# Two-layer pair block on one core: three gate banks copied out before their sigmoids, second-norm roots earlier, third-norm roots regrouped

## The reference

```python
# layer 0
x    = layernorm(pair) * ln1_w + ln1_b
left = sigmoid(x @ left1) * (x @ left2);  right = sigmoid(x @ right1) * (x @ right2)
p    = einsum('nsre,nkre->nske', left, right)
p    = layernorm(p) * ln2_w + ln2_b
g    = sigmoid(x @ gate)
x1   = pair + einsum('nrse,ez->nsrz', p, out_w) * g
# layer 1
left = (x1 @ W_left + b_left) + (x1 @ W_eq + b_eq)
rsum = sum over r of (x1 @ W_right + b_right)
out  = left * rsum * sigmoid(x1 @ W_gate + b_gate)
out  = out @ W_out + b_out
return layernorm(out + x1) * ln_scale + ln_bias
```

## Time and profile before

| | us |
|---|---|
| median of 3 runs | 116.27 |
| lowest and highest | 115.69, 116.97 |
| the profiled execution, its own time | 115.33 |
| its span, first to last instruction | 113.5 |
| TensorE busy in the span | 89.4 |
| VectorE busy | 78.8 |
| ScalarE busy | 69.5 |
| GpSimd busy | 63.0 |

### The profile page before, as it was taken

How to read it: one execution, slowest core, us unless ns; L and a number is a source line. 1 busy time by engine, 2 the same in 40 slices (tenths; PEclk the granted TensorE clock), 3 DMA queues, 4 the chain that set the end, 5 groups by cost and what they waited for, 6 DMA issues and landing times.

```text
span 113.5 us, 1817 instructions
## 1 busy us (share of the span) xinstructions
PE 89.4 (79%) x566; PEld 69.4 (61%) x566; DVE 78.8 (69%) x279; ACT 69.5 (61%) x118; POOL 63.0 (56%) x78
## 2 busy tenths in 40 slices
PE   1965993299999899976399999999999998894000
PEld 1954572257777699634063598988779896894000
DVE  1528698949978800399694558667799897999910
ACT  0614788748786256672289747987995997731100
POOL 5037983699970000007466549298843969984800
PEclk9999599859999999999999999999999999999855
DMA  3589995000000000000000000000000014639796
GB/s 60 112 138 166 146 146 50 0 0 6 0 0 0 3 6 0 0 0 3 0 0 0 0 9 0 0 0 0 0 0 6 0 28 64 92 58 144 107 145 101
DMA packets 33484, 4.51 MB, mean 40 GB/s; under 512 B 33348, under 2 KB 33476, under 8 KB 33476
## 3 DMA queue, kind: packets, MB, share of 16 engines
q1 hardware_dynamic: 31632, 4.00, 26.9%
q10 hardware_dynamic: 1844, 0.41, 1.8%
HBM read 2.31 MB, written 2.10 MB: 39 GB/s over the span
## 4 chain that ended last, share of the span: by engine, by line
PE 53%; DVE 15%; ACT 8%; issue 8%; DMA 5%; POOL 3%; SPq 2%; DVEq 0%; POOLq 0%
PE bank L793 9%; PE bank L835 7%; PE bank L923 6%; DMA x_tok<-in_x 5%; PE bank L846 5%; PE bank L932 5%; PE bank L881 5%; PE bank L778 3%; PE bank L870 3%; DVE lr L709 3%; PE bank L895 3%; PE bank L898 3%; PE bank L896 3%; DVE stats L573 3%; DVE lr L588 3%
## 5 line engine op out<-in xcount | busy, mean ns | idle before, releaser
L351 POOL TENSOR_TENSOR t_tok<-p_sb,rstd 128x512 f32<-128x512 f32 x7 | 10.2, 1452 | 19.6 <-DVE rstd L659 19.6
L793 PE MATMUL bank<-lr_blk,xnT 64*128 64x256 f32 x128 | 18.2, 425 | 2.3 <-ACT xnT L420 2.1
L588 DVE TENSOR_TENSOR lr<-bank,sig_lr 128x512 f32<-128x512 f32 x16 | 15.9, 1042 | 3.7 <-ACT sig_lr L430 3.6
L359 POOL TENSOR_TENSOR x_low<-x1T,x_high 128x512 fp32r<-128x512 f32 x8 | 11.0, 1379 | 9.4 <-ACT x_high L489 9.4
L793 PEld LDWEIGHTS bank<-lr_blk,xnT 64*128 64x128 f32 x128 | 12.6, 200 | 5.9 <-POOL lr_blk L298 1.9
L653 DVE BATCH_NORM_STATS2 stats<-p_sb 128x6 f32<-128x64 f32 x64 | 8.6, 212 | 7.6 <-ACT p_sb L464 7.6
L430 ACT ACTIVATE sig_lr<-bank 128x512 f32<-128x512 f32 x16 | 9.6, 597 | 5.0 <-PE bank L793 5.0
L573 DVE BATCH_NORM_STATS2 stats<-x_tok 128x6 f32<-128x64 f32 x64 | 9.0, 214 | 3.5 <-DMA x_tok<-in_x 3.3
L375 POOL TENSOR_TENSOR sq<-lr,row_rep 128x512 f32<-128x512 f32 x7 | 9.8, 1400 | 2.0 <-DVE lr L712 2.0
L367 POOL TENSOR_TENSOR oT<-o_a,rsum 128x512 f32<-128x512 f32 x8 | 8.7, 1088 | 3.6 <-ACT rsum L493 2.0
L692 DVE SCALAR_TENSOR_TENSOR o_a<-bank,leq_bias,sig 128x512 f32<-128x512 f32 x8 | 6.0, 748 | 6.1 <-ACT sig L501 2.9
(11 more groups left out here) (99 smaller groups left out, 201.2 us busy)
## 6 DMA issues: line engine op xcount, KB each, us to landing
x_tok<-in_x SPq DMA_DIRECT2D x14, 128.0 KB, 4.3
out<-sq SPq DMA_DIRECT2D x7, 256.0 KB, 3.3
x_tok<-in_x SPq DMA_DIRECT2D x3, 64.0 KB, 2.6
w_rep<-in_weights ACTq DMA_DIRECT2D x1, 180.5 KB
out<-sq ACTq DMA_DIRECT2D x1, 128.0 KB, 4.6
out<-sq SPq DMA_DIRECT2D x1, 128.0 KB, 4.9
x_tok<-in_x ACTq DMA_DIRECT2D x1, 64.0 KB, 2.7
row_rep<-in_rows ACTq DMA_DIRECT2D x1, 32.0 KB, 5.2
```

The costliest lines, as they stand in the source:

```text
L351: nc.gpsimd.tensor_tensor(place(t_tok[:, c % 2], 0, SPC), even_first(p_sb[:, :, s]), even_first(rstd[:, 1:2, s]).to_broadcast([P, 2, SPC / ...
L359: nc.gpsimd.tensor_tensor(x1_low[:, c % 2], x1T[:, c % 3], x1_high[:, c % 2], ALU.subtract).then_inc(x1_low_ready, 1)
L588: nc.vector.tensor_tensor(lr[:, :, s].rearrange("p f s -> p s f"), src[:, :, 2 * CH:4 * CH], sig_lr[:, j % 3].rearrange("p (s f) -> p s f" ...
L793: last = nc.tensor.matmul(dst, xnT[half, c, k * P:(k + 1) * P], lr_blk[half].rearrange("p g m c -> p g (m c)"), start=True, stop=True, ski ...
```

## The change

`GATE0_BANK` is changed, so that gate 4 uses bank 3 again and gate 5 bank 5. Gates 2, 3 and 4 (`RAW`) are copied raw from their banks to `gT` right behind `root2_of(0)` on ScalarE (`raw_gate0`, three more ACTIVATE of 128x512), and their Sigmoid later runs in place in `gT`. TensorE projects gates 4 and 5 ahead of the loop, gate 6 in turn 0, gate 7 in turn 1; the waits of `project_sums`, `project_1` and `centre_y` on the sigmoids are narrowed to the bank that each needs.

`root2_of(1)` stands ahead of `evacuate_tT(1)`, `root2_of(2)` directly behind it; on VectorE `statistics2(5)` stands ahead of `residual0(0)` and `inverse2(2)` in turn 1. `root2_of(3)` moves from turn 3 to turn 4, directly ahead of `root3_of(0)`, and `inverse2(3)` to the end of turn 4. The third-norm roots are regrouped (`ROOTS3`: six groups rather than five) and issued in turns 4, 6, 8 and 9 rather than 5, 7 and 9, and the one-column Sigmoid stands at the end of turns 4, 6 and 8 rather than 3, 5 and 7. `scale3(0)` is in turn 5 rather than 6, `bias3(0)` in 6 rather than 7.

```diff
--- before.py
+++ after.py
@@ -57,15 +57,16 @@
 ROOTS2 = [(0, 2), (2, 4), (4, 6), (6, 8)]
 
 
-GATE0_BANK = [3, 4, 6, 7, 5, 6, 7, 5]
-
-
-
-
-ROOTS3 = [(0, 2), (2, 4), (4, 6), (6, 7), (7, 8)]
-ROOT3_AT = {5: 0, 7: 1, 9: 2}
-SCALE_AT = {6: [0], 7: [1], 8: [2], 9: [3]}
-BIAS_AT = {7: [0], 8: [1], 9: [2, 3]}
+GATE0_BANK = [3, 4, 6, 7, 3, 5, 6, 7]
+RAW = (2, 3, 4)
+
+
+
+
+ROOTS3 = [(0, 1), (1, 3), (3, 5), (5, 6), (6, 7), (7, 8)]
+ROOT3_AT = {4: 0, 6: 1, 8: 2, 9: 3}
+SCALE_AT = {5: [0], 7: [1], 8: [2], 9: [3]}
+BIAS_AT = {6: [0], 8: [1], 9: [2, 3]}
 
 
 def place(tokens, lo, hi):
@@ -191,7 +192,7 @@
         tri_ps, p_ready = sem("tri_ps"), sem("p_ready")
         stats2_ready, root2, rstd2 = sem("stats2_ready"), sem("root2"), sem("rstd2")
         pool_step = sem("pool_step")
-        g_ps, g_ready = sem("g_ps"), sem("g_ready")
+        g_ps, g_raw, g_ready = sem("g_ps"), sem("g_raw"), sem("g_ready")
         t0_ready, t_ready, tT_ps, tT_ready = sem("t0_ready"), sem("t_ready"), sem("tT_ps"), sem("tT_ready")
         q_ps, xT_ps, x1_ready = sem("q_ps"), sem("xT_ps"), sem("x1_ready")
         rs_ps, rs_ready, l_ps, g1_ps, sig1_ready = (
@@ -463,9 +464,18 @@
                 src = bank[:, b].rearrange("p (e s) -> p e s", e=4)
                 nc.scalar.activation(p_sb[:, 4 * b:4 * b + 4, :], src, ACT.Copy).then_inc(p_ready, 1)
 
+            def raw_gate0(c):
+
+                act.wait_ge(g_ps, c + 1)
+                nc.scalar.activation(gT[:, c], bank[:, GATE0_BANK[c]], ACT.Copy).then_inc(g_raw, 1)
+
             def gate0(c):
-                act.wait_ge(g_ps, c + 1)
-                nc.scalar.activation(gT[:, c], bank[:, GATE0_BANK[c]], ACT.Sigmoid).then_inc(g_ready, 1)
+                if c in RAW:
+                    act.wait_ge(g_raw, RAW.index(c) + 1)
+                    nc.scalar.activation(gT[:, c], gT[:, c], ACT.Sigmoid).then_inc(g_ready, 1)
+                else:
+                    act.wait_ge(g_ps, c + 1)
+                    nc.scalar.activation(gT[:, c], bank[:, GATE0_BANK[c]], ACT.Sigmoid).then_inc(g_ready, 1)
 
             def root2_of(b):
                 first, last = ROOTS2[b]
@@ -475,6 +485,8 @@
             gate0(0)
             gate0(1)
             root2_of(0)
+            for c in RAW:
+                raw_gate0(c)
 
             def evacuate_tT(c):
                 act.wait_ge(tT_ps, c + 1)
@@ -513,14 +525,15 @@
                 root(2, ROOTS3[b][0] * SPC, ROOTS3[b][1] * SPC, root3)
 
             for i in range(CHUNKS + 3):
+                if i == 1:
+                    root2_of(1)
                 if i < CHUNKS and i != 2:
                     evacuate_tT(i)
                 if i == 1:
 
-                    root2_of(1)
+                    root2_of(2)
+                    evacuate_tT(2)
                     high1(0)
-                    evacuate_tT(2)
-                    root2_of(2)
                 if i == 2:
                     gate0(2)
                     gate0(3)
@@ -534,13 +547,13 @@
                 if i == 2:
                     for c in range(4, CHUNKS):
                         gate0(c)
-                if i == 3:
+                if i == 4:
                     root2_of(3)
                 if i in ROOT3_AT:
                     root3_of(ROOT3_AT[i])
                 if 0 <= i - 3 < CHUNKS:
                     evacuate_y(i - 3)
-                if i == 3 or i in ROOT3_AT and i <= CHUNKS:
+                if i in ROOT3_AT and i <= CHUNKS:
 
                     nc.scalar.activation(scratch[:], eps[:], ACT.Sigmoid)
             for b in range(len(ROOT3_AT), len(ROOTS3)):
@@ -722,14 +735,12 @@
 
             dve.wait_ge(out0_ready, 2)
             for i in range(CHUNKS + 2):
+                if i == 1:
+                    statistics2(5)
                 if 0 <= i - 1 < CHUNKS:
                     residual0(i - 1)
                 if i == 1:
-                    statistics2(5)
-                if i == 2:
                     inverse2(2)
-                if i == 4:
-                    inverse2(3)
                 if i <= CHUNKS:
                     for c in SCALE_AT.get(i, []):
                         scale3(c)
@@ -742,16 +753,18 @@
                 if i > CHUNKS:
                     for c in SCALE_AT.get(i, []):
                         scale3(c)
+                if i == 4:
+                    inverse2(3)
                 if i in ROOT3_AT:
                     inverse3(ROOT3_AT[i])
             scale3(4)
             variance3(6)
             scale3(5)
-            inverse3(3)
+            inverse3(4)
             variance3(7)
             dve.wait_ge(rstd3, len(ROOTS3) - 1)
             normalise3(6, 6 * SPC, 7 * SPC)
-            inverse3(4)
+            inverse3(5)
             lo = (CHUNKS - 1) * SPC
             dve.wait_ge(rstd3, len(ROOTS3))
             for h in (lo, lo + SPC // 2):
@@ -842,7 +855,11 @@
                 pe.wait_ge(p_ready, b + 1)
                 if b in GATE0_BANK[:c]:
 
-                    pe.wait_ge(g_ready, max(n for n in range(c) if GATE0_BANK[n] == b) + 1)
+                    last = max(n for n in range(c) if GATE0_BANK[n] == b)
+                    if last in RAW:
+                        pe.wait_ge(g_raw, RAW.index(last) + 1)
+                    else:
+                        pe.wait_ge(g_ready, last + 1)
                 nc.tensor.matmul(bank[:, b], gate0_blk[:], xnT[:, c], start=True, stop=True).then_inc(g_ps, 1)
 
             def transpose_x(c):
@@ -859,6 +876,8 @@
             for c in range(4):
                 project_gate0(c)
             transpose_x(0)
+            project_gate0(4)
+            project_gate0(5)
 
             def transpose_t(c):
                 if c == 0:
@@ -885,7 +904,7 @@
             def project_sums(m):
                 pe.wait_ge(x1_ready, 2 * BLK * (m + 1))
 
-                pe.wait_ge(rs_ready, m) if m else pe.wait_ge(g_ready, CHUNKS)
+                pe.wait_ge(rs_ready, m) if m else pe.wait_ge(g_ready, GATE0_BANK.index(RS) + 1)
                 nc.tensor.matmul(bank[:, RS, 0:2 * BLK], right_blk[:],
                                  x1_sum[:, 2 * m:2 * m + 2].rearrange("p c b -> p (c b)"), start=True, stop=True
                                  ).then_inc(rs_ps, 1)
@@ -908,6 +927,8 @@
                 project_split(c, G, 1, g1_ps)
                 if c:
                     pe.wait_ge(oa_ready, c)
+                else:
+                    pe.wait_ge(g_raw, len(RAW))
                 project_split(c, L, 0, l_ps)
 
             def centre_y(c):
@@ -916,8 +937,8 @@
                 b = Y + c % 2
                 if c >= 2:
                     pe.wait_ge(y_ready, c - 1)
-                elif c == 0:
-                    pe.wait_ge(g_ready, CHUNKS)
+                else:
+                    pe.wait_ge(g_ready, 7 + c)
                 for j in range(BLK):
                     k = slice(j * P, (j + 1) * P)
                     nc.tensor.matmul(in_order(bank[:, b], j), x1T[:, c % 3, k], centre_blk[:], start=j == 0, stop=False,
@@ -947,18 +968,17 @@
                 if i < CHUNKS:
                     transpose_t(i)
                 if i == 0:
-                    project_gate0(4)
+                    project_gate0(6)
                 if 0 <= i - 1 < CHUNKS:
                     project_q(i - 1)
+                if i == 1:
+                    project_gate0(7)
                 if i >= 3 and i % 2 and i - 2 < CHUNKS:
                     project_sums((i - 3) // 2)
                 if 0 <= i - 3 < CHUNKS:
                     centre_y(i - 3)
                 if 0 <= i - 2 < CHUNKS:
                     project_1(i - 2)
-                if i == 2:
-                    for c in range(5, CHUNKS):
-                        project_gate0(c)
                 if 0 <= i - 3 < CHUNKS:
                     project_y(i - 3)
             pe.wait_ge(out_scaled, 2)
```

## The result

The changed kernel took 119.35 us in the median (117.99 to 121.60, 4 runs), the kernel before beside it 115.98 us (114.45 to 116.97, 4 runs): ratio 1.027, 95% interval 1.018 to 1.035. The forecast was 118.7 us, slower. The ratios are taken over the faster executions of each kernel alone and the medians over all, so a ratio is not quite the quotient of its medians.

What follows compares the result with a forecast made beforehand. TensorE was taken to bound turns 3 to 9, with VectorE's tail behind `gate1(7)` setting the end. The terms -2.6 + 1.95 + 1.2 + 1.9 = +2.45 us on the 116.27 us median gave 118.7 us, range 115.6 to 120.4 us.

Steps and rivals of the forecast that it cites:

- Part 1: Gates off TensorE's path at the front: `centre_y(0)` at 62.9 instead of 65.5 us, gain 2.6 us (2.2 to 3.1).
- Part 2: Earlier second-norm roots: gives nothing more, since `project_1(0)` waits for `residual0(0)`, and costs 0.1 us.
- Part 3: Table pairs moved from odd to even turns: TensorE stalls or end later by 1.95, 1.2 and 1.9 us.
- Turn 5: Stall ahead of `project_y`, with two roots in the pair and `residual0(3)` late on VectorE: 1.95 us (1.4 to 2.1).
- Turn 7: Stall ahead of `project_y`: 1.2 us, from a chain of 9.1 us against TensorE's own 7.88 us.
- Turns 8 and 9: `gate1(7)` on ScalarE, and with it `gated1(7)` and the end, 1.9 us later (1.5 to 2.4).
- The 0.25 us of slack: Kernel before: `sums_of_right(1)` led to `times_right(2)`, ending at 77.61 us; TensorE asked for it at 77.86 us.
- A: Rival: the front's gain survives because table pairs cost TensorE nothing; 113.7 us, chance 0.11.
- B: Rival: the delays come half as large, as VectorE and GpSimd catch up; 116.2 us, chance 0.17.
- C: Rival: at the front, `transpose_t(0)` is pushed or sigmoids come later; gain 1.5 us or less, 119.8 us, chance 0.07.
- D: Rival: new stalls in `project_y` lower the clock, last matmuls up to 2.5 us more; 121.2 us, chance 0.05 with the drain.
- drain: By the page 2.66 us per table change, three pairs some 8 us more; the trace showed none. Chance 0.05 with D.

Runs made afterwards that it cites:

- e7_old_roots2: e1_old_third with the second norm's roots and statistics2(5) back in their old order, so only the gates' part is left; 114.74 us, ratio 0.991.
- e8_pair_in_turn8: e1_old_third with one table pair more, chunk 4's third-norm root and a one-column sigmoid in turn 8; 116.43 us against 116.50 for the kernel before, ratio 1.002.
- the best kernel: e1_old_third without the one-column sigmoid of turn 3, profiled twice; 114.38 us, then 114.66 us, ratio 0.989 to the kernel before.
- the second series: The changed kernel run again, unaltered, beside the kernel before; 119.39 us against 115.74 us, ratio 1.025.
- e1_old_third: The changed kernel with third-norm roots, `root2_of(3)`, `inverse2(3)` and one-column sigmoid back in their old turns; 114.17 us against 115.87 for the kernel before, ratio 0.980.

## Why the prediction was right

**Part 1** put `centre_y(0)` 2.6 us sooner; it is 2.56. The reason was right too: in the changed kernel its start falls on the end of the sigmoid of gate 6, and none of the raw copies is on the path.

**Part 2** was the step that failed: "gives nothing more, and costs 0.1 us". It is worth 0.75 us (e7_old_roots2), and the cost did not appear: `high1(0)` starts 10.79 us behind G0 in the changed kernel and 10.78 before. The gain was in the sum all the same, credited to part 1: the list of ScalarE's work from `high1(0)` to the sigmoid of gate 6 has the table load directly behind `high1(0)`, and that is only so because part 2 moves `evacuate_tT(2)` and `root2_of(2)` ahead of it. The gates alone bring `centre_y(0)` to 17.27, 1.81 us sooner. The prediction followed the data (who waits for the new roots) and not the queue (what the moved instructions no longer stand in front of).

**Part 3** was right in kind, place and number, and short by 0.9 us in all:

- Turn 5: 1.95 forecast, 2.16 measured.
- Turn 7: 1.2 forecast, 1.71 measured. The chain from the end of `project_q(5)` (78.59) to `project_y(4)` (88.07) took 9.48 us, not 9.1: 0.20 us from the end of `project_q` to the start of `residual0`, which the sum left out, the hand-over to `times_right` 0.13 for 0.03, `times_right` 1.13 for 1.05. The 2.0 us from `residual0` to `high1` was right (78.79 to 80.79). The left-out 0.20 us could be read before: the row that marks the end of `project_q(2)` there starts 0.20 us ahead of `residual0(2)` at 65.02 us. Another 0.1 us goes when TensorE restarts: `project_y(2)` behind the gap took 0.99 us to the next start, where it took 0.89 us without one.
- Turns 8 and 9: 1.9 forecast, 2.05 measured; the end follows `gate1(7)` one for one (e8_pair_in_turn8: 2.42 and 2.40).

The row before that marks the end of `project_q(2)`, and `residual0(5)` of the changed kernel:

```profile
64.82 0.60 PE L855 MATMUL bank<-ident,x_tok 128*128 128x128 f32 x4
```

```profile
78.79 0.75 DVE L689 SCALAR_TENSOR_TENSOR u<-bank,q_bias,gT 128x512 f32<-128x512 f32 x1 [1.80 <-PE bank L900]
```

The three delays come to 5.92 us, above the 5.7 that the forecast's range allowed (its lower end, 4.3, is not the sum of its parts either: 1.4, 1.2 and 1.5 are 4.1). By the traces the change costs 3.35 us where 2.45 was forecast. The time came closer than that, 118.7 against 119.35, partly by luck: the forecast started from a median of 116.27 us, which a fourth run brought to 115.98.

One reading of the prediction was wrong without harm: before, `times_right(2)` at 76.56 us did not wait for `sums_of_right(1)`, which had ended at 76.16, but for GpSimd's own `normalise2`. The 0.25 us of slack was that of GpSimd's queue.

The tail kept its length (11.71 and 11.72 us). Of the rivals, A is excluded by the gaps; B would have had each delay at half its size, and they are all above the forecast; C by `centre_y(0)`. D's mechanism exists, in another place than it was put: its fall at the last matmuls costs nothing, the one in turn 5 costs 1.6 us. The change of table cost 1.28 us everywhere and the next instruction began 0.01 us behind it (84.62 + 1.28, 85.91), so no drain appears here. The Trainium skill, "ScalarE: Activation LUTs", section "What ACT_TABLE_LOAD costs", adds a drain of about 1380 ns to every change of table; where the page and this trace differ, the trace decides.

## What to carry to other kernels

A table load has no fixed price; its price is what stands behind it in the queue. Here the same number of loads left TensorE busy all through the earlier trace rows in odd turns and put the end 5.5 us later in even ones. The next turn began with a small result (0.26 us of work) that GpSimd waits for and TensorE behind it, and at the end with the sigmoid that VectorE's tail starts from. Before a group of instructions is moved, write down the first urgent result behind it in both places, and add up the way to its reader against that reader's own way; and look at what the moved instructions no longer block, since that was worth more than their own results being early.

## What the runs showed of the hardware

The same instructions from the start to G0 took 45.16 to 48.01 us over these profiles, while the 59 us behind it repeated to 0.02 us in the two profiles of the best kernel (58.63 and 58.61), whose clock stayed up there. Part of the spread is the clock: the last work ahead of G0, the 64 matmuls of the einsum, took 7.41 us in the second series of the changed kernel, at a granted clock of 1.00 (40.0 to 45.1 us), and 8.99 us in e1_old_third, at 0.75. A difference of 2 us between two executions of such a kernel says nothing of an edit behind that point; a mark in the trace does.

The same stall of TensorE (1.96 and 1.97 us idle, same place, same instructions since G0) was followed by matmuls at 1.2 GHz in one execution and at 2.4 GHz in another. An fp32 matmul of 128 x 128 by 128 columns occupied TensorE for two rows of 0.11 us.
